# Cross-attention with two softmaxes: half-precision transposes of the high halves, and the low halves turned by paired DMA transposes

## The reference, cut to what matters

```python
q = heads(hidden_states @ W_q)
k_t, v_t = heads(text_ehs @ W_k), heads(text_ehs @ W_v)
probs_t = softmax(einsum('bhsd,bhtd->bhst', q, k_t) * attn_scale)
text_out = einsum('bhst,bhtd->bhsd', probs_t, v_t)
attn_scores = einsum('bhsd,bhnd->bhsn', q, heads(ip_ehs @ W_k_ip)) * attn_scale
qsem = _l2norm(einsum('bhst,bte->bhse', probs_t, text_ehs))
sem = einsum('bhse,bne->bhsn', qsem, _l2norm(ip_ehs))
probs_ip = softmax(attn_scores + 0.5 * sem) * spatial_mask
out = (text_out + einsum('bhsn,bhnd->bhsd', probs_ip, v_ip)) @ W_out + b_out + residual
```

## Time and profile before

| what | value |
|---|---|
| median of 3 runs | 740.36 us (739.94 to 740.94) |
| the profiled execution, its own time | 739.64 us |
| its span, first to last instruction | 736.4 us |
| mean granted TensorE clock | 0.993 |
| one batch in the steady stretch | 43.1 us |

### The profile page before, as it was taken

One profiled execution on the slowest core, in us unless ns is written; L12 is line 12 of the kernel. 1 busy time (PEld: TensorE's weight loads), 2 busy tenths in 40 slices (PEclk: granted clock), 3 DMA queues, 4 the chain that ended last, 5 costly groups with the idle time before them and its releaser, 6 DMA issues.

```text
span 736.4 us, 22506 instructions
## 1 busy us (share of the span) xinstructions
PE 715.9 (97%) x7215; PEld 562.2 (76%) x7215; DVE 634.7 (86%) x1878; ACT 558.0 (76%) x1591; POOL 416.9 (57%) x513
## 2 busy tenths in 40 slices
PE   7798999999999999999999999999999999999897
PEld 5477788787887878788787878878777887877664
DVE  4488998989889898988989898898989889898984
ACT  5378787887878788787878878787787878777770
POOL 7244647456564645656565555656555565654653
PEclk9999999999999999999999999999999999999999
DMA  9665363452636335263534526353352635234000
GB/s 283 125 163 105 78 129 78 64 130 55 125 75 125 82 61 140 46 126 74 111 98 62 124 55 131 75 115 93 58 115 72 127 75 106 51 56 102 10 7 16
DMA packets 137058, 68.56 MB, mean 93 GB/s; under 512 B 77056, under 2 KB 136880, under 8 KB 136944
## 3 DMA queue, kind: packets, MB, share of 16 engines
q1 hardware_dynamic: 132368, 64.39, 41.3%
q10 hardware_dynamic: 4576, 2.74, 1.4%
HBM read 40.38 MB, written 15.24 MB: 76 GB/s over the span
## 4 chain that ended last, share of the span: by engine, by line
PE 90%; DVE 3%; ACT 1%; DMA 1%; issue 1%; ACTq 1%; POOL 0%; SPq 0%; POOLq 0%; DVEq 0%
PE ps_prep L634 18%; PE ps_gram L741 18%; PE ps_pT L724 13%; PE ps_gram L742 12%; PE ps_score L716 6%; PE ps_prep L695 5%; PE ps_val L750 4%; PE ps_val L751 2%; PE ps_prep L692 1%; PE ps_prep L778 1%; PE ps_prep L665 1%; PE ps_prep L667 1%; PE ps_prep L789 1%; DMA w_raw<-in_L_xattn_W_k_ip 1%; PE ps_prep L782 1%
## 5 line engine op out<-in xcount | busy, mean ns | idle before, releaser
L564 POOL TENSOR_TENSOR dual<-prob 128x371 f32<-128x371 f32 (+1 forms) x288 | 251.0, 872 | 290.6 <-ACT prob L941 290.6
L741 PE MATMUL ps_gram<-gram_hi,pT_hi 125*128 125x371 f16 (+1 forms) x864 | 272.4, 320 | 0.1
L742 PE MATMUL ps_gram<-gram_lo,pT_hi 125*128 125x371 f16 (+2 forms) x864 | 230.1, 267 | 0.0
L935 ACT ACTIVATE pT_hi<-ps_pT 125x384 f16<-125x384 f32 (+1 forms) x288 | 138.8, 482 | 115.0 <-PE ps_pT L724 107.1
L1116 DVE TENSOR_TENSOR pT_lo<-ps_pT,pT_hi 125x384 f16<-125x384 f32 (+1 forms) x288 | 155.2, 539 | 31.8 <-ACT pT_hi L935 27.3
L925 ACT ACTIVATE prob<-ps_score,low 128x371 f32<-128x371 f32 (+1 forms) x288 | 165.4, 574 | 20.5 <-DVE low L1111 15.3
L1111 DVE TENSOR_REDUCE low<-ps_score 128x1 f32<-128x371 f32 (+1 forms) x288 | 154.9, 538 | 16.8 <-PE ps_score L716 11.7
L1129 DVE CUSTOM_DVE_ANT_0 quad_junk<-ps_gram,dual 128x371 f32<-128x371 f32 (+1 forms) x288 | 153.1, 532 | 3.6 <-PE ps_gram L742 0.8
L750 PE MATMUL ps_val<-val,pT_hi 125*128 125x84 f16 (+3 forms) x864 | 152.3, 196 | 0.0
L941 ACT ACTIVATE prob<-prob 128x371 f16<-128x371 f32 (+1 forms) x288 | 151.5, 526 | 0.0
L724 PE MATMUL ps_pT<-ident,prob 128*125 128x128 f32 (+1 forms) x864 | 142.0, 273 | 7.7 <-ACT prob L925 4.0
(11 more groups left out here) (214 smaller groups left out, 1466.8 us busy)
## 6 DMA issues: line engine op xcount, KB each, us to landing
ctx_sb<-in_ctx_t SPq DMA_DIRECT2D x15, 750.0 KB, 4.9
w_raw<-k_bounce SPq DMA_DIRECT2D x32, 216.0 KB, 3.9
k_st<-k_bounce SPq DMA_DIRECT2D x28, 216.0 KB, 3.8
k_bounce<-k_hi SPq DMA_DIRECT2D x15, 288.0 KB, 4.3
k_bounce<-k_lo SPq DMA_DIRECT2D x15, 288.0 KB, 4.3
q_st<-q_bounce SPq DMA_DIRECT2D x60, 63.0 KB, 2.4
xt_sb<-in_x_t SPq DMA_DIRECT2D x16, 168.0 KB, 5.3
k_st<-k_hi SPq DMA_DIRECT2D x32, 84.0 KB, 3.2
```

The lines of the kernel that those rows point to most:

```text
L564: nc.gpsimd.tensor_tensor(dual[0:r, t % 2, :], prob[0:r, g % 4, 0:TX], prob_16[0:r, t % 2, :], ALU.subtract).then_inc(s_dual, 1)
L741: nc.tensor.matmul(ps_gram[t % 2][:, 0:TX], hi, gh[0:TROWS[i], i, :], start=(i == 0), stop=False, skip_group_check=True)
L742: last = nc.tensor.matmul(ps_gram[t % 2][:, i * TC:TX], hi, gl[0:TROWS[i], i, i * TC:TX], start=False, stop=(i == NT - 1), skip_group_chec ...
```

## The change

Blocks 0 to 13 are now turned in two ways. ScalarE makes `prob_16`, the float16 rounding of the block (scale 1.0 in place of 0.5), as the first thing of its step t for block t+2. TensorE turns `prob_16` with three float16 transposes into the same bank, read as float16. GpSimd makes the low half in its own new instruction, `low_probs` (`prob` minus `prob_16`, as float16), two steps ahead, into `prob_lo`, which holds two pairs of blocks. A DMA transpose on the SyncE queue, `turn_lo`, turns a pair of low halves (128 rows by 6 times 128 columns) into `turned_lo`, which holds three pairs. The VectorE instruction `probs_lo` is left for blocks 14 to 17 alone, which keep the float32 transposes.

The value products are taken out of `products` and run later, pair by pair, when the turned low halves are there: blocks 2q and 2q+1 at step 2q+3, blocks 12 to 15 at step 15, 16 and 17 at their own. `low_probs` of a pair waits for the transfer of the pair two before; `turn_lo` waits for the values of the pair three before. GpSimd still makes `dual` for every block, from `prob` and `prob_lo` by an addition in blocks 0 to 13, and the constant of the norm changes with it. The finishing steps of the last batch, and the move of rows, come two steps later.

```diff
-GROUPS = ((0, 6), (6, 12), (12, NBX), (NBX, NB))
+GROUPS = ((0, 6), (6, 12), (12, NB))
+EVACS = ((0, 6), (6, 12), (12, NBX), (NBX, NB))
+EVAC_STEP = {7: 0, 13: 1, 15: 2, 17: 3}
+VALUES_AT = {**{2 * q + 3: (2 * q, 2 * q + 1) for q in range(6)}, 15: (12, 13, 14, 15), 16: (16,), 17: (17,)}
+HI_SLOTS, X_SLOTS, LO_PAIRS, TURNED_PAIRS = 5, 4, 2, 3
-EARLY = NBX
+EARLY = 12
-VALS_STEP, POW_STEP, EXP_STEP = 0, 2, 6
+VALS_STEP, POW_STEP, EXP_STEP = 2, 4, 8
-... LOAD_X_STEP, MOVE_OUT_STEP, MOVE_IN_STEP = 2, 3, 4, 7, 8, 12, 14, 15
+... LOAD_X_STEP, MOVE_OUT_STEP, MOVE_IN_STEP = 2, 3, 4, 7, 8, 12, 16, 17
 # SyncE
+            def turn_lo(b, q):
+                n = pair(b, 2 * q)
+                sp.wait_ge(s_prob_lo, lows_to(b, 2 * q + 1))
+                if n >= TURNED_PAIRS:
+                    past = n - TURNED_PAIRS
+                    sp.wait_ge(s_val, NB * (past // PAIRS) + 2 * (past % PAIRS) + 2)
+                sp.dma_start_transpose(turned_lo[:, n % TURNED_PAIRS, :, :],
+                                       prob_lo[:, n % LO_PAIRS, :, :, :].rearrange("s a c t -> s (a c t)")).then_inc(s_turned[n % TURNED_PAIRS], 16)
             def body(b, prepare, turning, finishing):
                 for t in range(NB):
+                    if t % 2 and t < NBX - 2:
+                        turn_lo(b, (t + 1) // 2)
+                    if prepare and t == NB - 1:
+                        turn_lo(b.next(), 0)
                     if turning and t == 0:
 # GpSimd
+            def low_probs(b, t):
+                g, n = NB * b.n + t, pair(b, t)
+                pool.wait_ge(s_prob_16, g + 1)
+                if t % 2 == 0 and n >= LO_PAIRS:
+                    past = n - LO_PAIRS
+                    pool.wait_ge(s_turned[past % TURNED_PAIRS], 16 * (past // TURNED_PAIRS + 1))
+                nc.gpsimd.tensor_tensor(prob_lo[:, n % LO_PAIRS, t % 2, :, 0:TC], chunks(prob[:, g % 4, :]), chunks(prob_16[:, g % X_SLOTS, :]),
+                                        ALU.subtract).then_inc(s_prob_lo, 1)
             def duals(b, t):
-                pool.wait_ge(s_prob_16, g + 1)
                 reached(pool, s_quad, g - 1)
-                nc.gpsimd.tensor_tensor(dual[0:r, t % 2, :], prob[0:r, g % 4, 0:TX], prob_16[0:r, t % 2, :], ALU.subtract).then_inc(s_dual, 1)
+                if t < NBX:
+                    pool.wait_ge(s_prob_lo, lows_to(b, t))
+                    nc.gpsimd.tensor_tensor(chunks(dual[:, t % 2, :]), chunks(prob[:, g % 4, :]), prob_lo[:, pair(b, t) % LO_PAIRS, t % 2, :, 0:TC],
+                                            ALU.add).then_inc(s_dual, 1)
...
                 for t in range(NB):
+                    if t + 2 < NBX:
+                        low_probs(b, t + 2)
+                    elif prepare and t + 2 >= NB:
+                        low_probs(b.next(), t + 2 - NB)
 # TensorE
             def transposes(b, t):
-                pe.wait_ge(s_prob, g + 1)
-                reached(pe, s_pT_lo, g)
+                if t < NBX:
+                    pe.wait_ge(s_prob_16, g + 1)
+                    src, out_, unit = prob_16[0:r, g % X_SLOTS, :], ps_pT[:, :].bitcast(F16), ident_16
...
+                    gram_products(b, t)
+                    for u in VALUES_AT.get(t, ()):
+                        value_products(b, u)
 # value_products(b, t), ahead of the matmuls
+                if t < NBX:
+                    n = pair(b, t)
+                    if t % 2 == 0:
+                        pe.wait_ge(s_turned[n % TURNED_PAIRS], 16 * (n // TURNED_PAIRS + 1))
+                    lo = turned_lo[:, n % TURNED_PAIRS, t % 2 * NT:(t % 2 + 1) * NT, :]
 # ScalarE
                 for t in range(NB):
+                    if t + 2 < NB:
+                        halve(b, t + 2)
+                    elif prepare:
+                        halve(b.next(), t + 2 - NB)
                     if t + 1 < NB:
                         probs_hi(b, t + 1)
...
-                    if t + 1 < NB:
-                        halve(b, t + 1)
 # VectorE
-                    if t + 1 < NB:
+                    if NBX <= t + 1 < NB:
                         probs_lo(b, t + 1)
```

148 lines of the change are left out of this document (84 added, 64 removed).

## The result

The changed kernel takes 891.8 us (median of 4 runs, 888.1 to 893.4) where the kernel before takes 740.2: a ratio of 1.204, 95% interval 1.200 to 1.208. Slower, as forecast, but by 152 us where 31 were forecast, and outside the range. The profiled execution has a span of 889.7 us.

The account below looks back on a forecast made before the run. TensorE's own work was taken as the bound, 43.1 us a batch. 739.64 + 15 batches x (3.3 wait + 0.8 clock - 1.96 won) - 1.96 + 1 = 770.8, forecast 771 us; likeliest case 757 to 804, full range 718 to 830.

Parts of the forecast that it names:

- what the change wins: On TensorE, 14 blocks' transposes go from 0.33 to 0.19 us each: 1.96 us a batch won.
- the end: In the tail, the move of rows comes two steps later: 1 us counted, between 0 and 2.
- a last batch of 2 us less: Sign of being right: the last batch has no restacking, so pairs land in time and 1.96 us stay won.
- where TensorE would stand: TensorE waits 3.3 us a batch for pair 3 at step 9; pair 5's wait at step 13 is already covered.
- Pair 1 is issued ahead of the q stores; its 0.9 us fits into the 1.03 us in which the queue now waits: On SyncE's queue, pair 1's transpose fits into the existing wait between the two q stores.
- L: Time from a DMA transpose's issue to its landing: 3.8 us taken, bounds 1.6 to 5.3.
- X: Time one DMA transpose holds the SyncE queue: 0.9 us taken, bounds 0.30 to 1.70.
- GpSimd's wait at step 8: GpSimd's low half of block 10 waits for pair 3's landing; costed at nothing, with thin cover.
- It isn't the bound, so I cost this at nothing: VectorE loses 14 remainders, 7.7 of its 38.65 us a batch; costed at nothing.
- The clock: TensorE's halt may halve its clock: 0.8 us a batch counted, bounds 0 and 1.5.
- GpSimd becomes the bound: Rival: GpSimd's 37.4 us of work a batch plus its wait at step 8 set the time, 783 us; chance 0.04.
- Costlier transposes: Rival: DMA transposes cost more than plain transfers; 877 us if six serial pieces, 840 with upper bounds; chance 0.12.

Follow-up runs that it names:

- Experiment 9: Changed kernel without DMA transposes or waits for them, low products reading zeros, VectorE's fprob, text_lo, nrm and fused instructions reading one tile: 709.6 us, ratio 0.960.
- experiment 2: Changed kernel with four slots for pairs of low halves in place of two: 847.9 us, ratio 1.146.
- experiment 4: Changed kernel with DMA transposes and GpSimd's waits kept, but TensorE's low products read zeros and wait for nothing: 913.2 us, ratio 1.233.
- experiment 3: Changed kernel with the DMA transposes and the waits for them taken out, low products reading a tile of zeros: 798.4 us, ratio 1.078.
- experiment 13: Changed kernel, own queue order and two slots, with VectorE's fprob, text_lo, nrm and fused instructions reading one tile: 848.2 us, ratio 1.147.
- experiment 12: Changed kernel with 38 Gram products added on TensorE at step 9, filling its wait for pair 3: 902.6 us, ratio 1.219.

## Why the prediction was right or wrong

*Right: what the change wins.* 1.96 us a batch and 1 us for the end gave 710 us for a kernel without a wait. Experiment 9, in which TensorE waits for no pair and VectorE isn't held (and parts are left out), took 709.6. A block's transposes came down from 0.33 to 0.17, by the columns, a little better than the row for turning the Gram matrix that I had taken. The sign "a last batch of 2 us less" failed: from its first score to the end of the span the last batch took 58.1 us (from 831.59) where it had taken 51.5 (from 684.86); 2.5 of that is a longer wait of TensorE for `fprob` (3.77 us up to 880.17, 1.26 before).

*Right: where TensorE would stand.* One wait a batch for a pair, at step 9, none at steps 3, 5, 7; the wait at step 13 covered by the first. I had worked out that TensorE would want pair 3 at 21.26 us; it did at 21.30.

*Wrong: "Pair 1 is issued ahead of the q stores; its 0.9 us fits into the 1.03 us in which the queue now waits".* I asked what stands behind a transpose, not what the transpose itself waits for, and pair 0 isn't in the sum at all. It stands at step 17 of the batch before and waits there for its low half, 4.4 us in nearly every batch, with the moved rows and the loads of context and x behind it; in the kernel before, the moved rows had gone out at 591.41, 7 us before the next batch began, and the two loads right behind them. So the queue was not free when q_hi was made (412.44, 3.67 us in, about when I had counted on it). Pair 1 followed at 413.72, and the store of q_hi at 6.25 us in place of 3.9. The entries from there to pair 3 took 0.5 us longer than I had counted (the extra pieces of q alone 6.5 us in place of 5.1), and pair 3 went out at 23.59, not 20.75: 2.84 of the 3.7 us by which the wait was mis-sized. The rest is the landing: some 4.7 us after its issue (437.04 - 432.36) for L = 3.8. The issue time X had a median of 1.24 us for 0.9, and pair 3's own was 1.90 in this batch. The median of L, 3.6, was well hit; pair 3's wasn't. The Trainium skill, page "VectorE: DVE Perf Modes", section "The three transpose paths", had led to an estimate of 7.9 us for a pair (the sum with it is 833 us, not 834); the trace doesn't bear that out. The Trainium skill's page "Advanced Engine Details and Errata", section "X-Bar Transpose (TRN2)", says that such transfers are as fast as plain ones, and for the landing the trace agrees: 3.6 us for 192 KB beside 3.8 and 4.0 for the 216 KB loads of k. What cost most was the time in the queue.

*Wrong: "I cost it at nothing; the cover is thin", of GpSimd's wait at step 8.* It cost some 2.0 to 2.9 us a batch (experiment 2), and had TensorE not waited at all it would have cost the whole wait over again (experiment 4).

*Wrong, and the largest miss: VectorE, "It isn't the bound, so I cost this at nothing".* I counted the 7.7 us that it loses and never asked what GpSimd's 12.3 us more would do to it. They hold VectorE's instructions with two inputs in SBUF, 88.8 us over the kernel when nothing else is wrong (experiments 3 and 9). Beside the transposes it adds 44 (experiment 13 against the changed kernel), since part of it lies under TensorE's wait. There was a sign of it: in the kernel before, one VectorE instruction of 14 columns had a mean of 0.81 us beside 0.16 for the same one with 6 columns, which its size doesn't explain:

```profile
L1142 DVE TENSOR_SCALAR nrm<-nrm 112x14 f32<-112x14 f32 x16 | 13.0, 810 | 0.0
```

In all 14 batches in which it took over 0.5 us it ended within 0.03 us of the end of a GpSimd instruction (`dual`), so this was the hold already, as far as a trace can show it. The Trainium skill, page "SBUF — State Buffer", section "Who interferes with whom", says that a VectorE instruction with two SBUF inputs contends with a GpSimd instruction that reads SBUF. That rule spoke against the change, and I didn't weigh it; the 0.34 us of `fprob` that became 2.86 in experiment 3 agree with it.

*The clock.* Half clock came as in the setup, for about 10 us (432 to 442), 5 of which had work (4.96 busy), so some 2.5 us and not the 0.8 that I counted. But experiment 12 shows that in this kernel it wasn't a cost of its own: without it, the time goes to the wait for `fprob`, which comes 7.6 us after the landing either way.

*The rivals.* "GpSimd becomes the bound" had the right engine for the wrong reason: its 37 us fit (experiment 9); what costs is that its instructions follow one another beside VectorE's. "Costlier transposes" gave 840 and 877 by a longer landing; in fact it's mostly their time in the queue and their waiting there. A range whose upper end was made only of X and L, 830, couldn't hold two mechanisms that I had put at nothing.

## What to carry to other kernels

An in-order queue has two prices for each new entry: its issue time, and the time for which it waits for its own input while everything behind it stands; work out when the input of each entry is made, not only where the entry stands. Before work is given to an engine that "has room", list what the engines beside it share with it: the instructions of VectorE that read two tiles of SBUF paid here for GpSimd's work, and the first sign is an instruction whose mean is far above what its size explains. Two waits that end together hide each other, so a wait costed at nothing should be costed once more with its cover taken away.
